# Expert passes and an edge network in one GNN kernel: where biases are added, how rows are turned, and which operand of a sum is loaded

## The reference

```
# L1: mixture of experts, 3 layers, h is 6250 x 256
h = x @ W_in + b_in
for l in range(3):
    agg    = segment_sum(h[src], dst) / deg
    logits = concat([h, agg]) @ router_W[l] + router_b[l]        # 8 experts, top 2, softmax -> gate
    weak   = relu(agg @ weak_W[l] + weak_b[l])                   # 4 experts, 256 -> 256
    strong = relu(agg @ strong_W1[l] + strong_b1[l]) @ strong_W2[l] + strong_b2[l]   # 4 experts, 256 -> 512 -> 256
    h      = h + sigmoid(h @ conf_W[l] + conf_b[l]) * sum(gate * experts)
out = h @ W_out + b_out
# L2: edge network
theta = x[dst] - x[src]
w     = sigmoid(relu(theta @ W1 + b1) @ W2 + b2)
out   = segment_sum(w * theta, dst) + indeg * (x @ W4 + b4)
```

## Time and profile before

| | |
|---|---|
| median of 3 runs | 7931.63 us (7931.56 to 7933.56) |
| the profiled execution | 7939.88 us, span 7938.1 us |
| TensorE busy | 7037.5 us (89% of the span) |
| VectorE / ScalarE / GpSimd busy | 3745.6 / 2117.7 / 3287.4 us |
| pass 1, about | 1266 to 2505 us of the span |
| pass 2, about | 2513 to 3753 us |
| pass 3, about | 3761 to 5184 us |
| edge network, about | 5196 to 6507 us |
| mean granted clock of TensorE | 0.870 of full speed |

### The profile page before, as it was taken

The page is one execution under the profiler, slowest core; times in us unless marked ns, Lnnn a source line. Parts: engine busy times, 40 slices in busy tenths (PEclk is TensorE's granted clock), DMA queues, the critical chain, the costliest instruction groups (busy, mean ns, idle before and its releaser), DMA issues. The chain is left out here.

```text
span 7938.1 us, 153720 instructions
## 1 busy us (share of the span) xinstructions
PE 7037.5 (89%) x52426; PEld 5001.9 (63%) x52426; DVE 3745.6 (47%) x10518; ACT 2117.7 (27%) x6385; POOL 3287.4 (41%) x3380
## 2 busy tenths in 40 slices
PE   0788885999997999998899999879999978989899
PEld 0455554888886888886677777656666644545455
DVE  5999973444443444443344444356666651121111
ACT  1444441222221222222333333312222210000000
POOL 0000005666664666664655656356666640000000
PEclk6899997999998999999999999955555559999999
DMA  3333334555554555553555545344444437646564
GB/s 105 95 111 113 117 125 146 162 161 161 163 161 133 166 160 161 162 161 109 176 143 141 144 138 145 102 111 128 127 127 128 126 99 238 196 160 196 177 194 159
DMA packets 688444, 1156.88 MB, mean 146 GB/s; under 512 B 251592, under 2 KB 488812, under 8 KB 685618
## 3 DMA queue, kind: packets, MB, share of 16 engines
q0 software_dynamic: 200640, 601.97, 27.5%
q1 hardware_dynamic: 440242, 415.44, 17.3%
q10 hardware_dynamic: 46784, 129.65, 4.6%
HBM read 958.31 MB, written 188.49 MB: 144 GB/s over the span
## 5 line engine op out<-in xcount | busy, mean ns | idle before, releaser
L609 POOL DMA_INDIRECT ring<-parts,idx x2496 | 2416.6, 968 | 1431.2 <-issue 708.0
L2208 PE MATMUL agg_ps<-sheet,big 128*128 128x448 f16 x6174 | 1195.6, 354 | 36.2 <-DMA sheet<-adj 36.2
L1193 PE MATMUL y<-big,strong 128*128 128x256 f32 x4704 | 1172.5, 392 | 0.0
L1232 PEld LDWEIGHTS hid<-agg,big 128*128 128x128 f32 x9408 | 1116.7, 192 | 48.8 <-issue 37.9
L1232 PE MATMUL hid<-agg,big 128*128 128x128 f32 x9408 | 1136.6, 276 | 0.0
L609 POOL DMA_INDIRECT ring<-rows_yh,idx x832 | 819.4, 985 | 571.5 <-PE sums L753 257.3
L1125 ACT ACTIVATE strong<-hid,s_b 128x128 f32<-128x128 f32 x2352 | 671.5, 368 | 1183.5 <-PE hid L1232 1183.5
L2208 PEld LDWEIGHTS agg_ps<-sheet,big 128*128 128x128 bf16 x6174 | 605.7, 99 | 584.6 <-DMA sheet<-adj 38.7
L1193 PEld LDWEIGHTS y<-big,strong 128*128 128x128 f32 x4704 | 845.2, 189 | 161.8
L734 DVE TENSOR_TENSOR acc<-acc,sums 128x128 f32 (+1 forms) x832 | 222.3, 267 | 1383.7 <-PE sums L753 1353.7
L2018 POOL MEMSET acc<- 128x6400 f32 x4 | 21.7, 5432 | 1970.0 <-POOLq L85 1007.9
(11 more groups left out here) (373 smaller groups left out, 8134.9 us busy)
## 6 DMA issues: line engine op xcount, KB each, us to landing
sheet<-adj SPq DMA_DIRECT2D x294, 784.0 KB, 4.2
ring<-parts,idx POOLq DMA_INDIRECT x2496
adj<-big ACTq DMA_DIRECT2D x7, 5488.0 KB
adj<-acc ACTq DMA_DIRECT2D x7, 5488.0 KB
relb<-rel_rows ACTq DMA_DIRECT2D x106, 256.0 KB, 4.1
parts<-cut SPq DMA_DIRECT2D x99, 192.0 KB, 1.8
h<-rows SPq DMA_DIRECT2D x147, 128.0 KB
ring<-rows_yh,idx POOLq DMA_INDIRECT x832
```

Of the source, the lines that this page charges most:

```text
L609: nc.gpsimd.indirect_dma_start(ring[:, k, :], None, table, bass.IndirectOffsetOnAxis(ap=idx[:, h, c:c + 1].bitcast(U32), axis=0),).then_in ...
L1193: ins = nc.tensor.matmul(y, s["strong"][:, e % 2, k, :], w["s2"][:, k, e, :], start=False, stop=(k == 3))
L1232: ins = nc.tensor.matmul(p["hid"][:, bank_at, j * P:(j + 1) * P], w["s1"][:, k, e, j * P:(j + 1) * P], s["agg"][:, k, :], start=(k == 0), ...
L2208: last = nc.tensor.matmul(ps[:, g % 2, 0:HALF_COLS], now[:, b, c, :], sheet[:, k, s * HALF_COLS:(s + 1) * HALF_COLS], start=(b == 0 and c ...
```

## The change

1. **Biases.** The bias matmuls of `weak` and `down` are gone, and with them `bias`, `ones3`, `bias_dram` and the phase that cut the biases. `weak_b` and `down_b`, broadcast to 128 partitions (512 KB each), are loaded in each pass's prologue. VectorE adds `weak_b` from PSUM into `weak` (`biased0`, `biased1`), ScalarE's relu then works in place, and `up1`, `up2` wait for these adds instead of the relu. VectorE adds gate x `down_b` to the row in four multiply-adds (`down_b0` to `down_b3`) ahead of `mix0`.
2. **Turns.** `h` also comes as three bf16 parts (`hp`, a third load of 192 KB a block), and the two float32 transposes are six bf16 matmuls with a bf16 identity.
3. **Edge-network sums.** The weighted one-hot (64 columns) is loaded and the ring's rows with a 129th column of ones move, one matmul a tile into `by_target`. The sum has targets on partitions, so ScalarE copies it (`copy_sums`) and TensorE turns it back (`turn_sums`, two small float32 matmuls), one group later; VectorE's adds to `acc` come one group later as well (`add_sums`).
4. `Layer2`'s block work starts four tiles later in its step (`BEGIN = 4`).

```diff
+                ring = tmp.enter_context(sbuf("ring", [P, RING, YH + 1], FP) if edge_net
                                          else sbuf("ring", [P, RING, PARTS * width], B16))
                 onehot = tmp.enter_context(sbuf("onehot", [P, 2, HALF, WIN], FP if edge_net else B16))
...
+                        def copy_sums(n):
+                            act.wait_ge(tiles_done, RING + GROUP * (n + 1))
+                            if n >= 2:
+                                act.wait_ge(sem["turned"], n - 1)
+                            nc.scalar.copy(held_sums[:, n % 2, :], by_target[:, n % 2, 0:D + 1]).then_inc(sem["copied"], 1)
                         def stage(i, h, col):
...
                         if loop == "edges":
...
+                            if edge_net:
+                                if i * GROUPS + g >= 1:
+                                    add_sums(i * GROUPS + g - 1)
+                                return
...
+                        def add_sums(n):
+                            w = dve.value_load(win[0:1, bass.ds(n, 1)], min_val=0, max_val=SPARE)
+                            dve.wait_ge(sem["turned"], n + 1)
+                            dve.wait_ge(added, n + 2)
+                            nc.vector.tensor_tensor(acc[0:1, 1, bass.ds(w, WIN)], acc[0:1, 1, bass.ds(w, WIN)],
+                                                    sums[0:1, n % 2, WIN:2 * WIN], ALU.add)
+                            nc.vector.tensor_tensor(acc[:, 0, bass.ds(w, WIN)], acc[:, 0, bass.ds(w, WIN)],
+                                                    sums[:, n % 2, 0:WIN], ALU.add).then_inc(added, 1)
...
+                        def turn_sums(n):
+                            pe.wait_ge(sem["copied"], n + 1)
+                            pe.wait_ge(added, n + 2)
+                            nc.tensor.transpose(sums[:, n % 2, 0:WIN], held_sums[:, n % 2, 0:D], ident[0:WIN, 0:WIN])
+                            nc.tensor.matmul(sums[0:1, n % 2, WIN:2 * WIN], held_sums[:, n % 2, D:D + 1], ident[0:WIN, 0:WIN],
+                                             start=True, stop=True).then_inc(sem["turned"], 1)
...
+                            n = i * GROUPS + g
+                            if q == 2 and n >= 1:
+                                turn_sums(n - 1)
...
-                            pe.wait_ge(added, i * GROUPS + (g + 1))
-                            pe.wait_ge(sem["weighted"], i * GROUPS + (g + 1))
+                            if n >= 2:
+                                pe.wait_ge(sem["copied"], n - 1)
+                            pe.wait_ge(sem["weighted"], n + 1)
                             for j in range(GROUP):
-                                hot = onehot_w[:, g % 2, j, :]
-                                tile_sum(sums[:, g % 2, 0:WIN], ring[:, g * GROUP + j, D:YH], hot, j == 0)
-                                last = tile_sum(sums[0:1, g % 2, WIN:2 * WIN], ones[:, 0:1], hot, False, j == GROUP - 1)
+                                last = nc.tensor.matmul(by_target[:, g % 2, 0:D + 1], onehot_w[:, g % 2, j, :],
+                                                        ring[:, g * GROUP + j, D:YH + 1], start=(j == 0), stop=(j == GROUP - 1))
...
+            DVE = ("agg biased0 logits_sb top topi topf diff neg_conf biased1 plus1 recips gate0 gate1 pick0 pick1 gates "
+                   "down_b0 down_b1 down_b2 down_b3 mix0 mix1 mix2 mix3 mix4 mix5")
...
+                s["hp"] = tmp.enter_context(sbuf("hp", [P, PARTS * H], B16))
...
-                self.loads(m, [(s["h"][:, :], rows_of(rows256[self.cur], b)), (s["rdeg"][:, :], rdeg_dram[:, bass.ds(b * P, P)])])
+                self.loads(m, [(s["h"][:, :], rows_of(rows256[self.cur], b)), (s["rdeg"][:, :], rdeg_dram[:, bass.ds(b * P, P)]),
+                               (s["hp"][:, :], rows_of(parts256[self.cur], b))])
...
-                    m.need(self.pe, f"weak{q}")
-                    m.need_before(self.dve, f"mix{2 * q + 1}")
-                    m.done(f"relu_w{q}", nc.scalar.activation(s["weak"][:, 2 * q:2 * q + 2, :],
-                                                              p["hid"][:, q, :].rearrange("p (e f) -> p e f", f=H), ACT.Relu))
+                    m.need(self.dve, f"biased{q}")
+                    both = s["weak"][:, 2 * q:2 * q + 2, :]
+                    m.done(f"relu_w{q}", nc.scalar.activation(both, both, ACT.Relu))
...
+                def biased(q):
+                    m.need(self.pe, f"weak{q}")
+                    m.done(f"biased{q}", nc.vector.tensor_tensor(
+                        s["weak"][:, 2 * q:2 * q + 2, :], p["hid"][:, q, :].rearrange("p (e f) -> p e f", f=H),
+                        self.w["weak_b"][:, 2 * q:2 * q + 2, :], ALU.add))
+                biased(0)
...
+                biased(1)
...
+                for e in range(NW):
+                    self.mix(m, f"down_b{e}", row, self.w["down_b"][:, e, :], NW + e, row if e else s["h"][:, :])
+                m.need(self.act, "relu_w0")
+                self.mix(m, "mix0", row, s["weak"][:, 0, :], 0, row)
...
-                nc.tensor.matmul(y, w["ones3"][0:PARTS, :], w["bias"][0:PARTS, NW * H + e * H:NW * H + (e + 1) * H], start=True,
-                                 stop=False)
                 for k in range(4):
-                    ins = nc.tensor.matmul(y, s["strong"][:, e % 2, k, :], w["s2"][:, k, e, :], start=False, stop=(k == 3))
+                    ins = nc.tensor.matmul(y, s["strong"][:, e % 2, k, :], w["s2"][:, k, e, :], start=(k == 0), stop=(k == 3))
...
-                    ins = nc.tensor.transpose(p["route"][:, a * P:(a + 1) * P], s["h"][:, a * P:(a + 1) * P], ident[:, :])
+                    for c in range(PARTS):
+                        ins = nc.tensor.matmul(p["route"][:, a * P:(a + 1) * P], s["hp"][:, c * H + a * P:c * H + (a + 1) * P],
+                                               w["ident16"], start=(c == 0), stop=(c == PARTS - 1))
...
-                    nc.tensor.matmul(hid, w["ones3"][0:PARTS, :], w["bias"][0:PARTS, q * 2 * H:(q + 1) * 2 * H], start=True,
-                                     stop=False)
...
-                        m.need(self.act, f"relu_w{e - 1}")
+                        m.need(self.dve, f"biased{e - 1}")
...
+            BEGIN = 4
...
-                go(w["bias"][:, :], bias_dram[l, :, :])
+                go(w["weak_b"][:, :, :].rearrange("p e f -> p (e f)"), bcast_vec(t["L1_gnn_weak_b"][l, :, :].rearrange("e f -> (e f)")))
+                go(w["down_b"][:, :, :].rearrange("p e f -> p (e f)"), bcast_vec(t["L1_gnn_strong_b2"][l, :, :].rearrange("e f -> (e f)")))
...
```

More of the change, by code:

```diff
@@ L63 @@
 PARTS = 3
+LAST_GROUP = TURNS * GROUPS - 1
 YH = 2 * D
@@ L518, in edge_pass @@
                 idx = tmp.enter_context(sbuf("idx", [P, 2, HALF], I32))
-                sums = tmp.enter_context(psum("sums", [P, 2, 512]))
+                sums = tmp.enter_context(psum("sums", [P, 2, 256 if edge_net else 512]))
                 bufs = work.buffers(tmp)
@@ L533, in edge_pass @@
                     zt = tmp.enter_context(psum("zt", [P, 2, GROUP, P]))
+                    by_target = tmp.enter_context(psum("by_target", [WIN, 2, 512]))
+                    held_sums = tmp.enter_context(sbuf("held_sums", [WIN, 2, D + 1]))
                     names += ["rel_loaded0", "rel_loaded1", "z_done", "net_own", "dot_done", "weight_done",
-                              "weighted"] + [f"ywin_loaded{g}" for g in range(GROUPS)]
+                              "weighted", "copied", "turned"] + [f"ywin_loaded{g}" for g in range(GROUPS)]
                 def programs(block, sems, loop):
@@ L609, in _ @@
                                 nc.gpsimd.indirect_dma_start(
-                                    ring[:, k, :], None, table,
+                                    ring[:, k, 0:YH] if edge_net else ring[:, k, :], None, table,
                                     bass.IndirectOffsetOnAxis(ap=idx[:, h, c:c + 1].bitcast(U32), axis=0),
@@ L663, in _ @@
                                     load_window(0, k)
-                        over(act, tile)
+                        over(act, tile, flush=(lambda: copy_sums(LAST_GROUP)) if edge_net else None)
                         if edge_net and loop == "edges":
@@ L743, in _ @@
                             if loop == "edges":
+                                nc.vector.memset(ring[:, :, YH:YH + 1], 1.0)
                                 dots(0, 0)
-                            over(dve, tile, lambda i, k: tile(i, k, ahead=False))
+                            over(dve, tile, lambda i, k: tile(i, k, ahead=False), lambda: add_sums(LAST_GROUP))
                         else:
@@ L814, in _ @@
                         if edge_net:
-                            over(pe, net_tile, lambda i, k: net_tile(i, k, ahead=False))
+                            over(pe, net_tile, lambda i, k: net_tile(i, k, ahead=False), lambda: turn_sums(LAST_GROUP))
                         else:
@@ new lines, in expert_tables, with _ @@
```

(12 more changed lines are left out.)

82 lines of the change are left out of this document (22 added, 60 removed).

## The result

The changed kernel takes **7740.2 us** (median of 4 runs, 7738.3 to 7748.1) where the kernel before takes 7931.7: a ratio of 0.9759 (95% interval 0.9746 to 0.9771), 191.5 us faster. The prediction was 7781 us. In the first and third call of experiments the kernel before took 7935.1 and 7933.9 us; in the second it took 8591.0 us. The three calls ran on three chips, so each run is read by its ratio within its own call.

What follows compares the result with a forecast made beforehand. TensorE was taken to bound passes 1 and 2, a closed chain pass 3, and the gather the changed edge network; -145 + 190 - 201 + 5 = -151 us on 7939.9, adjusted to the median: 7781 us, range 7600 to 7930.

Steps and rivals of the forecast that it cites:

- 1.48 us a block: Passes 1 and 2: TensorE time freed by removing six bias matmuls; over 98 blocks, -145 us.
- That edit is a draw.: Expert passes: turning h by six bf16 matmuls costs TensorE 0.35 us, the same as two float32 transposes.
- The third load: Pass 3: loading hp delays agg by 1.2 us a block, between 0.5 and 1.8.
- The h2_t stall: Pass 3: TensorE's wait before h2_t grows from 0.78 to 3.1 us, with 2.07 us from the four new multiply-adds.
- The h_t stall: Pass 3: TensorE's wait before h_t becomes some 2.3 us, from 0.75 us before.
- The clock: Pass 3: slower work after long stalls, 1.64 us in about four blocks of five, +64 us.
- rival (b): Edge network: round trip, stretched by table loads and block work, holds about 5.8 us a group; -100 for -201; chance 0.12.
- (a): Pass 3: VectorE's adds and the third load hide, TensorE's saving counts; -73 for +190, 7518 us; chance 0.15.
- (c): Edge network: round trip takes 6.3 us a group or more, no gain there; 7982 us; chance 0.10.
- (d): Passes 1 and 2: VectorE's four two-input adds block the gather; -39 for -145, 7887 us; chance 0.05.
- (e): Pass 3: both clock drops are paid in each block; +283 for +190, 7874 us; chance 0.08.
- Small things: Bias setup -9, broadcast bias loads +10, blocks behind a pass waiting for the third load +4; sum +5 us.

Runs made afterwards that it cites:

- turn_f32: Changed kernel with h turned by two float32 transposes again and without the third load (hp): ratio 0.9604 to the kernel before.
- bias_128_rows_again: Kernel before with all bias matmuls kept, their operands zero-padded from 3 to 128 partitions, third call: ratio 0.9724, 217.6 us faster.
- three_gathers_of_four: Changed kernel leaving out every fourth tile's gather in the edge network from the second turn on: ratio 0.9754, edge network 1148.0 against 1155.1 us.
- edge_only: Kernel before with only the edge-network part of the change (sums and Layer2's later start), second call: ratio 0.9916, edge network 1369.3 us.
- small_gathers: Changed kernel with 16 rows instead of 128 in every fourth edge-network gather, second call: ratio 1.0130, edge network 1379.5 us.

## Why the prediction was right, and where it was wrong

**Passes 1 and 2: -145 predicted, -209 measured.** The limit was right: TensorE stays busy for 957.72 of 980 us. The term that was mis-sized is "1.48 us a block". I priced a bias matmul from its start to the next start, 0.21 and 0.32 us. The runs show 0.32 for `down` (2.83 - 2.51), and 0.39 for the first `weak` (from the turn, 2916.07, to the next group at 2918.56 it was 2.49 us, now 3013.62 - 3011.52 = 2.10). The 0.39 is what is left after the dearer turn: turn_f32, which has the two float32 transposes of before, takes 1.94 us, so this bias matmul cost about 0.55 us. A third of the cost of `down`'s lay in the neighbours' time. The row at 2918.56, timeline of before:

```profile
2918.56 0.51 PE L1244 MATMUL misc<-router,ht 128*128 128x9 f32 x4
```

bias_128_rows_again shows the same from the other side. By the block (800 us of pass 2 hold 33 blocks before and 36 after) the saving is 2.0 us; 98 x 2.0 = 198. I put the rest of the 209 down to the passes' ends, where I had expected +14: the gather's wait at the start of a pass is shorter by 7 to 10 us, not longer.

**"That edit is a draw."** Wrong by 0.16 us a block. My 0.35 us for the float32 transposes ended at the first 3-partition bias matmul, so the change of tile was in it; without such a neighbour they take 0.22.

**Pass 3: +190 predicted, +205 measured.** The chain was seen rightly. down_b in front: 2.07 x 48 = 99 predicted without the clock, 117 measured. The third load: +1.2 us predicted, 3.45 - 2.20 = 1.25 measured. The h2_t stall: 3.1 predicted, 2.78 measured. The h_t stall: 2.3 predicted, 3.45 measured. There the starting value failed first: I took 0.75 us from one block, and over the window it is 1.26. The growth was too small as well: 2.19 us measured (3.45 - 1.26), where my terms have 0.63 + 1.2 = 1.83 and the sum says 2.3 for their 2.6. The third load's 1.25 fits, so it is the other term that came out larger, 0.94 us (2.20 - 1.26) for 0.63. The clock: a block became 205.2/48 = 4.3 us longer although TensorE has 2.0 us less to do, so 6.3 us were added. The two waits grew by 2.2 + 2.4 = 4.6, and 1.7 are left, 80 us in pass 3 for the 64 predicted. The busy time says that they are the clock's. Window of the whole pass 3, before:

```profile
3762.08:5196.23 1434.15, 1300.07 (x11313) 1024.73 (x11313) 587.18 (x2130) 522.21 (x1476) 800.42 (x833) 0.95 0.49 139
```

TensorE's busy time fell by only 15 us (1300.07 to 1285.07), although some 98 us of work (49 x 2.0) were gone: the same work ran about 83 us slower, at a granted clock of 0.90 for 0.95.

**The edge network: -201 predicted, -184 measured.** The size was nearly right: 5.32 us a group for 5.24. The sums were priced rightly too: 412.1 us for 832 tiles are 0.50 us a tile for the 0.47 that I took (429 ns is the mean of one record, and a tile has two that overlap). The limit that I named was wrong: the gather, at 5.24 us a group, was to set the pace. Groups by line, whole span of the changed kernel:

```profile
L612 POOL DMA_INDIRECT ring<-rows_yh,idx x832 | 841.0, 1011 | 359.9 <-issue 250.0
...
L818 PE MATMUL by_target<-ring,onehot_w 128*64 128x129 f32 x1664 | 412.1, 429 | 0.8 <-DVE onehot_w L726 0.8
```

In the trace GpSimd goes back to back, and it waits for TensorE only 12.4 us of 1000. That looks like the limit. But in the waits of the same stretch (5250 to 6250 us, 188 groups) TensorE waits for a gather only 1.1 us; it waits for ScalarE and VectorE:

```profile
PE sums L797 <- ACT held_sums L640: 90.9, 60, 2.4
...
PE pb L1496 <- ACT wsum L1461: 37.7, 33, 1.9
...
PE pc L1503 <- DVE ht L1475: 19.9, 33, 0.9
```

These are 148.5 us of the 161 that TensorE stands idle. So a group is 4.46 us of TensorE's work (839.07/188) and 0.86 us in which it is idle. 0.48 us of that (90.9/188) is the round trip of rival (b), in about a third of the groups, and 0.31 us (57.6/188) are waits in Layer2's block work; for all unevenness I had allowed 0.1 us. In the round shown under three_gathers_of_four the table load, which I had only named, holds the sigmoid, and the block's `h` the copy; without block work a group takes 3.88 us, close to the 3.9 that I had for the round trip. The gather's own floor, 4 x (1.011 + 0.30) = 5.24 us, lies within 2% of the 5.32. That the size came out is therefore luck: it was worked out from a limit that three_gathers_of_four shows not to be the limit. Which link to shorten for a faster edge network was not tried, so what sets the 5.32 us is read from the waits and not shown by a run.

**The rivals.** (a): as changed, VectorE's adds and the third load did not hide in pass 3. The third load does once the loads are early, and the four multiply-adds do once they stand behind `mix3`. (c) did not come: the round trip stays under 6.06 us. (d) did not come either. The mean gather of the expert passes went from 968 to 983 ns, 15 ns x 17 = 0.26 us a block, where the rival had 2.1. By "SBUF — State Buffer" of the Trainium skill, under "Who interferes with whom", a VectorE instruction with two SBUF inputs contends with a GpSimd one that reads SBUF and not with one that only writes it; the same section infers that making a gather's descriptors needs the write side, so by that page rival (d) had little for it. The trace agrees: four such adds a block left the gather within 15 ns. (e) did not come: pass 3 lost 205 us and not 283.

**Small things:** setup -8.7 us for the -9 predicted (from the memset of `acc` to the first gather 66.6 us before, 57.9 after).

**The signs.** In pass 3 `agg` waited 241.1 us for its loads and TensorE 2.78 us before h2_t, and in the edge network TensorE was busy 4.46 us a group, as forecast. One sign of being wrong appeared in the edge network, where the mean gather is 1011 ns, above 1 us (983 ns in the expert passes). Another appeared in part: TensorE waited for `held_sums` in 60 of 188 groups.

**The sum** was 50 us too high by the profiled executions (41 us by the medians): passes 1 and 2 gave 64 us more than predicted and the small things 18 more (-13 for +5), while pass 3 cost 15 more and the edge network gave 17 less. The errors partly cancel, and the nearness of the total owes something to that.

## What to carry to other kernels

Price a small matmul of another shape by a stretch that holds its neighbours, from the group before it to the group behind it; its own start-to-start row showed 0.21 us of the 0.32 that it cost. Where a chain over several engines closes, an instruction that is only early in program order stands in it: moving four multiply-adds from in front of `shift` to behind `mix3` gave 117 us. Asking for the loads ahead of the wait for `next_h` gave 215.6 us, more than twice what leaving the third load out gave. A cheaper form of what is there is worth trying before it is moved to another engine: padding the bias matmuls gained 217.6 us and taking them off TensorE, with the rest of the change, 191.5. An engine that runs back to back is the limit only if another one waits for it.

## What the runs showed of the hardware

A bias matmul of 256 columns with a 3-partition operand between 128-partition ones costs 0.32 us at the 2.4 GHz level (2.83 - 2.51) where a padded one costs 0.03 (2.54 - 2.51); padding alone gave 217.6 us. An indirect gather costs GpSimd nearly the same for 16 rows (0.85 us) as for 128 (0.95).

The second call was slower only in the edge passes; its first two dense layers took 475 and 464 us (edge_only), like those of the other calls. In pass 2 TensorE stood idle with nothing that the profile could name in front of it. Timeline of TensorE, pass 2 of edge_only in that call:

```profile
2910.24 0.28 PE L777 MATMUL sums<-onehot,ring 128*128 128x64 bf16 x4 [0.43 <-issue]
2911.68 0.22 PE L777 MATMUL sums<-onehot,ring 128*128 128x64 bf16 x2 [1.16 <-issue]
2912.38 0.19 PE L777 MATMUL sums<-onehot,ring 128*128 128x64 bf16 x1 [0.48 <-issue]
...
2914.52 0.21 PE L777 MATMUL sums<-onehot,ring 128*128 128x64 bf16 x1 [1.16 <-issue]
```

Pass 2 as changed took 1477.4 us there (small_gathers), as before 1455.9 (edge_only): its saving was gone, and small_gathers as a whole was 1.3% slower than the kernel before. Groups of 24 sums, 0.70 us elsewhere, were torn apart in steps of some 0.7 us. Between 2900 and 3700 us such idle time is 51 us, while the 28 blocks in that stretch (33 before) stand for about 120 us lost; the rest is not explained. That TensorE lacked instructions, as the expectations of the third call have it, is a guess from "issue"; no run tested it. The changed kernel itself was not run there, so its verdict holds for the chips on which the kernel before takes about 7932 us.
